# Postnorm attention block on one core: two blocks of row maxima worked in the prologue, and maxima turned on TensorE straight from their columns

## The reference, cut to what matters

```python
def reference(h, gamma, beta, Wq, bq, Wk, bk, Wv, bv, Wo, bo, w_gate, w_up, w_down):
    hn = (h - mean(h)) * rsqrt(var(h) + 1e-05) * gamma + beta      # h: (2, 2048, 256)
    q, k, v = hn @ Wq + bq, hn @ Wk + bk, hn @ Wv + bv             # 16 heads of 64
    q, k = rope(q), rope(k)
    attn = softmax(where(tril, q @ k.T / 8, -inf))                 # per head, 2048 x 2048, causal
    x = layernorm(h + (attn @ v) @ Wo + bo + h)
    return layernorm(x + (silu(x @ w_gate.T / 127) * (x @ w_up.T / 127)) @ w_down.T / 127)
```

## Time and profile before

| | |
|---|---|
| median of 3 runs | 2232.11 us (2231.62 to 2236.57) |
| profiled execution, its own time | 2229.82 us |
| its span, first to last instruction | 2228.0 us |
| mean granted TensorE clock | 0.979 |
| PE busy | 2070.0 us, 93% |
| DVE busy | 1597.6 us, 72% |
| POOL busy | 1391.7 us, 62% |
| ACT busy | 906.6 us, 41% |

### The profile page before, as it was taken

The page is one execution under the profiler, slowest core; times in us unless marked ns, Lnnn a source line. Parts: engine busy times, 40 slices in busy tenths (PEclk is TensorE's granted clock), DMA queues, the critical chain, the costliest instruction groups (busy, mean ns, idle before and its releaser), DMA issues.

```text
span 2228.0 us, 37497 instructions
## 1 busy us (share of the span) xinstructions
PE 2070.0 (93%) x14720; PEld 1287.2 (58%) x14720; DVE 1597.6 (72%) x2262; ACT 906.6 (41%) x1245; POOL 1391.7 (62%) x1204
## 2 busy tenths in 40 slices
PE   6779999999999989999999999999999989889997
PEld 5445555555555545555555555555555545789996
DVE  8576878686878776767777777778787763556654
ACT  4424443444444434434343434343434345434342
POOL 1457777777787866677767777878787879000000
PEclk9899999999999999999999999999999999999999
DMA  6311212121202122122111212121112131231300
GB/s 223 119 30 38 62 39 62 39 62 39 58 25 68 42 68 72 45 65 63 48 53 43 58 43 58 43 58 34 48 34 58 29 119 48 67 104 57 112 10 29
DMA packets 116149, 132.16 MB, mean 59 GB/s; under 512 B 15248, under 2 KB 71184, under 8 KB 115728
## 3 DMA queue, kind: packets, MB, share of 16 engines
q1 hardware_dynamic: 115984, 129.92, 19.5%
HBM read 56.47 MB, written 39.85 MB: 43 GB/s over the span
## 4 chain that ended last, share of the span: by engine, by line
PE 60%; DVE 24%; DMA 5%; SPq 4%; issue 4%; ACT 1%; POOL 1%; ACTq 0%; DVEq 0%
PE o_ps L1239 13%; DVE mpart L833 9%; PE m_ps L1184 7%; DMA rot<-qr 5%; PE s_ps L1205 4%; SPq L385 4%; PE s_ps L1209 4%; PE s_ps L1207 4%; PE s_ps L1211 4%; PE x_ps L1139 3%; DVE qr L860 3%; PE x_ps L1246 3%; DVE qc L871 2%; PE gu_ps L1139 2%; PE gu_ps L1140 2%
## 5 line engine op out<-in xcount | busy, mean ns | idle before, releaser
L542 POOL TENSOR_TENSOR acc<-acc,pt 128x512 f32<-128x512 f32 (+3 forms) x1024 | 1195.8, 1200 | 228.0 <-ACT pt L591 228.0
L591 ACT ACTIVATE pt<-s_ps 128x1024 f32<-128x1024 f32 (+3 forms) x640 | 544.8, 895 | 704.8 <-PE s_ps L1211 342.4
L833 DVE TENSOR_REDUCE mpart<-m_ps 128x2 f32<-128x1024 f32 (+2 forms) x576 | 624.9, 1085 | 288.2 <-PE m_ps L1184 215.7
L1239 PE MATMUL o_ps<-pt,v 128*64 128x512 f32 (+3 forms) x2560 | 547.5, 549 | 0.0
L1184 PE MATMUL m_ps<-qk 64*128 64x512 f32 (+3 forms) x1280 | 290.0, 449 | 85.0 <-DVE mpart L833 73.7
L1184 PEld LDWEIGHTS m_ps<-qk 64*128 64x128 f32 x1280 | 121.1, 185 | 395.6 <-DVE mpart L833 223.6
L1239 PEld LDWEIGHTS o_ps<-pt,v 128*64 128x64 f32 x2560 | 157.8, 138 | 239.1 <-issue 213.8
L537 POOL TENSOR_TENSOR acc<-pt 128x512 f32<-128x512 f32 (+1 forms) x128 | 161.7, 1283 | 193.7 <-ACT pt L591 193.7
L1205 PE MATMUL s_ps<-qk 64*128 64x512 f32 (+3 forms) x1280 | 253.7, 392 | 0.0
L1209 PE MATMUL s_ps<-qk 64*128 64x512 f32 (+3 forms) x1280 | 235.6, 363 | 0.0
L1211 PE MATMUL s_ps<-aux,ones_r 64*128 64x512 f32 (+3 forms) x1280 | 234.7, 362 | 0.0
(11 more groups left out here) (165 smaller groups left out, 2882.0 us busy)
## 6 DMA issues: line engine op xcount, KB each, us to landing
rot<-qr SPq DMA_DIRECT2D x512, 64.0 KB, 2.0
attn<-o_sum SPq DMA_DIRECT2D x64, 256.0 KB, 2.3
o_raw<-attn SPq DMA_DIRECT2D x8, 2048.0 KB, 8.9
v<-v_far SPq DMA_DIRECT2D x16, 768.0 KB, 5.2
v_far<-v_part SPq DMA_DIRECT2D x48, 256.0 KB, 2.0
w_raw<-in_wqkv SPq DMA_DIRECT2D x34, 128.0 KB, 5.1
v_far<-v SPq DMA_DIRECT2D x16, 256.0 KB, 2.4
v<-v_far SPq DMA_DIRECT2D x16, 256.0 KB, 5.0
```

What stands on the lines that cost most here:

```text
L542: nc.gpsimd.tensor_tensor(sums, sums, probs, ALU.add).then_inc(summed, 1)
L591: nc.scalar.activation(pt[:, u % SLOTS, :, q0:NB], s_ps[:, two:two + 2, q0:NB], ACT.Exp, scale=SCALE)\
L833: nc.vector.tensor_reduce(dst, m_ps[:, :, 0:w], AX.X, ALU.max, negate=True).then_inc(maxed, 1)
L1239: last = nc.tensor.matmul(o_ps[rows, q0:NB], v[par][:, j, rows], pt[:, u % SLOTS, a, q0:NB], start=(j == 0), stop=(j == n - 1), skip_group ...
```

## The change

In words: `PROLOGUE_MAXIMA = 12`: the prologue works 12 steps of maxima of the first pair (blocks 0 and 1) in place of 4, and the first pair has 2, 2, 2, 3, 3, 2, 2, 3, 3, 3, 3 left in groups 0 to 10. The first four stand between the v tiles of the last chunk, the other eight between the turns of the second batch's input. In the first pair the third step of a group stands behind the other work, as in the other pairs. The remainders of the prologue (18 instructions) go from DVE to POOL; the rows of batch 1 (16) from POOL to ACT, which needs the negated mean times the inverse deviation (`next_mean`) from DVE. The order of input loads, of PE's chunks and of ACT's steps is changed to fit; ACT loads its first table at once. The copy `spread` and `mz` are gone: `turn_maxima` multiplies by the identity with the column of `mc`, repeated 64 times, as stationary operand, one matmul for each tile and head half, and `ones_r` holds 1/64, since all 64 rows now hold the maximum.

```diff
+PROLOGUE_MAXIMA = 12
+FIRST_COUNT = [2, 2, 2, 3, 3, 2, 2, 3, 3, 3, 3]
...
-                return FIRST_MAXIMA[g]
+                return range(PROLOGUE_MAXIMA + sum(FIRST_COUNT[:g]), PROLOGUE_MAXIMA + sum(FIRST_COUNT[:g + 1]))
...
-            load_input(0)
+            load_input(0, 0)
...
             load_w(0)
+            load_input(0, 1)
             load_wv(0, wv_raw[:, :])
             load_wv(1, v_part[:, :])
+            load_input(0, 2)
+            load_input(0, 3)
...
-            pool.wait_ge(a_rstd, len(STAT_TILES))
-            for t in range(TT):
-                next_rows(t)
+            rest(0)
+            rest(1)
+            rest_wv(0, wv_raw[:, :])
+            rest_wv(1, v_part[:, :])
+            for i in range(2, TURNS):
+                rest(i)
+            for c in range(BLOCKS):
+                remainders(c)
...
+            def next_rows(g):
+                act.wait_ge(next_shift, 1)
+                for t in range(TG * g, TG * (g + 1)):
+                    nc.scalar.activation(h_all[1][:, t, :], h_all[1][:, t, :], ACT.Identity,
+                                         bias=next_mean[:, t:t + 1], scale=rstd[:, TT + t:TT + t + 1])\
+                      .then_inc(next_norm, 1)
...
             rounded(1)
+            next_rows(0)
+            next_rows(1)
             evict_v_first(3)
             rounded(2)
+            shifts(0, 0)
+            next_rows(2)
+            next_rows(3)
+            next_affine(0)
+            next_affine(1)
             rounded(3)
...
-            nc.vector.memset(ones_r[:, :].bitcast(F32), 1.0).then_inc(out_stored, 16)
+            nc.vector.memset(ones_r[:, :].bitcast(F32), 1.0 / DK).then_inc(out_stored, 16)
...
-                    if turns and kind is not FIRST:
-                        spread(it + 1 if g == NG - 1 else it, TURN_M[g])
...
-                    late = 2 if kind is not FIRST else len(ms)
-                    for m in ms[:late]:
+                    for m in ms[:2]:
...
-                    if turns and kind is FIRST:
-                        spread(it + 1 if g == NG - 1 else it, TURN_M[g])
...
             def turn_maxima(n, blk):
-                pe.wait_ge(mz_done, n * BLOCKS + (blk + 1))
+                if blk == 0:
+                    pe.wait_ge(maxed, n * NM + TG)
+                else:
+                    pe.wait_ge(m_rows, n * (TT - TG) + TG * blk)
                 for t in range(TG):
-                    last = nc.tensor.transpose(x_ps[:, t * P:(t + 1) * P], mz[:, t, :], id_f[:, :])
+                    for a, rows in enumerate(halves):
+                        last = nc.tensor.matmul(x_ps[rows, t * P:(t + 1) * P], mc[:, blk, t, a:a + 1].broadcast_to([P, DK]),
+                                                id_f[:, :], start=True, stop=True, skip_group_check=True)
...
+            turn_chunk(0)
+            turn_chunk(1)
+            project_qk(0)
+            for c in range(3):
+                for t in range(TG * c, TG * (c + 1)):
+                    project_v_first(t)
+                if c < 2:
+                    turn_chunk(c + 2)
+                project_qk(c + 1)
             pe.wait_ge(cos_done, 6)
             pe.wait_ge(const_in, 16 * 6)
             for m in range(TG):
-                if m > 0:
-                    pe.wait_ge(maxed, m)
-                maxima(0, 0, m)
-            project_chunk(3)
+                first_maximum(m)
+                project_v_first(3 * TG + m)
             pe.wait_ge(v_done, TT - 1)
             turn_maxima(0, 0)
-            for i in range(TURNS, 2 * TURNS):
-                turn_input(i)
+            for m in range(TG, PROLOGUE_MAXIMA):
+                first_maximum(m)
+                turn_input(TURNS + m - TG)
```

More of the change, by code:

```diff
@@ L458, in _ @@
                 sp.dma_start(dst, src).then_inc(const_in, 16)
-            load_input(1)
+            for g in range(GROUPS):
+                load_input(1, g)
             sp.wait_ge(primed, 1)
@@ L470, in _ @@
                     load_b(1, 1)
+            for done in v_put:
+                sp.wait_ge(done, 16 * BLOCKS)
+            load_v(0, 0, 3, v_in)
             for c in range(BLOCKS):
@@ L688, in rounded @@
                     piece_hi(0, c, a, 0)
+            nc.scalar.activation(pause_act[:, :], ones_f[:, 0:1], ACT.Sqrt)
             root_input(0)
-            root_input(1)
-            weights(0, first=True)
-            root_input(2)
             act.wait_ge(ln_in, 16 * 3)
             affine(0)
+            weights(0, first=True)
             affine(1)
+            root_input(1)
             split_wv(0, wv_raw[:, :])
@@ L911, in pair @@
                 for g in range(NG):
-                    turns = g in TURN_M and (g != NG - 1 or kind is not LAST)
-                    if turns and kind is not FIRST:
-                        spread(it + 1 if g == NG - 1 else it, TURN_M[g])
                     ended = EVICTED.get(g) if g != 1 or kind is not FIRST else None
@@ L939, in pair @@
                         turned_sum(it + 1, *PIECE[g - 1])
-                    for m in ms[late:]:
+                    for m in ms[2:]:
                         maximum(it, m) if m < NM else maximum(it + 1, m - NM)
@@ L967, in turned, with next_means, first_maxima @@
                     turned_sum(0, c, a)
-            def remainders(c):
-                for a in range(2):
-                    piece_lo(0, c, a, 0)
+            def next_means():
+                dve.wait_ge(a_rstd, len(STAT_TILES))
+                nc.vector.scalar_tensor_tensor(next_mean[:, :], mv[:, TT:2 * TT, 0], -1.0, rstd[:, TT:2 * TT],
+                                               ALU.mult, ALU.mult).then_inc(next_shift, 1)
+            def first_maxima(a, b):
+                for m in range(a, b):
+                    maximum(0, m)
             input_group(0)
+            input_rows(0)
             input_group(1)
-            input_rows(0)
+            input_rows(1)
             weights(0)
             input_group(2)
-            input_rows(1)
-            rest(0)
-            rest(1)
-            rest_wv(0, wv_raw[:, :])
-            rest_wv(1, v_part[:, :])
-            input_group(3)
             input_rows(2)
-            rest(2)
-            rest(3)
-            input_rows(3)
             dve.wait_ge(const_in, 16 * 6)
             unturned(0)
+            input_group(3)
+            input_rows(3)
+            turned(0)
+            unturned(1)
             input_group(GROUPS)
             input_group(GROUPS + 1)
-            turned(0)
-            rest(4)
-            rest(5)
-            unturned(1)
+            turned(1)
             input_group(GROUPS + 2)
@@ L998, in _ @@
             input_var(GROUPS)
-            turned(1)
-            rest(6)
-            rest(7)
-            remainders(0)
+            unturned(2)
             input_inv(GROUPS)
-            unturned(2)
-            for m in range(TG):
-                maximum(0, m)
+            next_means()
+            first_maxima(0, 2)
             turned(2)
-            remainders(1)
-            spread(0, 0, first=True)
+            first_maxima(2, TG)
             unturned(3)
+            first_maxima(TG, TG + 2)
             turned(3)
-            remainders(2)
-            remainders(3)
+            first_maxima(TG + 2, PROLOGUE_MAXIMA)
             each_pair(dve, pair)
```

96 lines of the change are left out of this document (44 added, 52 removed).

## The result

The changed kernel takes 2206.57 us (median of 4 runs, 2196.1 to 2210.59) against 2231.86 for the one before: a ratio of 0.9882, interval 0.9849 to 0.9916, 25 us less. The prediction said 2207. Timed again with more runs it took 2202.73 us against 2227.36, ratio 0.9888 (0.9865 to 0.9911). The total agrees with the forecast, but not for the reasons that it gave: two of its terms were off by some 10 us each way, and that they cancel is luck.

The account below looks back on a forecast made before the run. PE bounds the kernel, by its own work in middle pairs, while the first pair loses over 20 us to waits. 5.3 + 15 + 2.4 + 0.5 = 23.2 us off 2229.8 gives 2206.6, said as 2207; 8 in 10 between 2193 and 2224.

Parts of the forecast that it names:

- Part 1: Prologue up to group 1 of the first pair: 5.3 us saved, bounds 0 and 10.
- the walk through the first rows: Start of the prologue, walked by durations: rows at about 14.3 us, first projection at 16.2, 1.3 us earlier.
- sixteen rows on ACT: Prologue: ACT's 16 rows of 256, 0.38 us each, lie beside the eight steps of maxima.
- the late prologue: Rival: POOL's sums or the turned-sum chain delay the first pair to 80 us or later; costs 6 to 8 us, chance 0.13.
- Part 2: First pair, groups 2 to 10: 15 us saved, 75.0 to 60 us, bounds 8 and 21; groups 13 and 15 add 2.4.
- the four steps fewer: First pair, groups 2 to 10: 28 steps become 24, each costing a round of 1.82 us, 7.3 us saved.
- The late step: First pair: third step behind other work saves 4 us of 7.9 at most, plus 2.4 in groups 13 and 15.
- In groups 0 and 1 the four steps: First pair's start: 4 steps instead of 8, some 1.6 us less each, 16.8 us becoming 10.4.
- Part 3: The 64 turns: 23.0 us added on PE, 23.5 given back, 0.5 us saved; bounds 13.5 lost and 12 gained.
- The price of the turn: PE's new turn takes 0.94 to 0.96 us against 0.58: 0.36 us more each, 23 us over 64 turns.
- what comes back there: Turns of blocks 2 and 3, 14 middle pairs: 23.5 us given back by the missing copy, including 9.5 of `qc` waits.
- cover: Turns of blocks 2 and 3: long waits for maxima behind the turn hide its 0.36 us, some 5 us.

Follow-up runs that it names:

- the first trace: The changed kernel, profiled in its fastest run: 2196.1 us, mean clock 0.987.
- copy_back: The changed kernel with DVE's copy and PE's transposes put back, prologue and first pair as changed: 2222.44 us, ratio 0.9961.
- direct_turn: The changed kernel, but DVE's reduction writes the two heads' maxima 64 columns apart and PE turns them with four transposes, no copy: 2187.29 us, ratio 0.9819.
- rest_dve: The changed kernel with the remainders of the input and v weights (10 instructions) back on DVE, those of q and k on POOL: 2204.71 us, ratio 0.9878.
- the second trace: The changed kernel unaltered, run once more and nearer to its usual run: median 2202.73 us (2197.59 to 2209.97).
- four_steps: The changed kernel with 4 steps of maxima in the prologue again, and in groups 0, 1 and 5 all steps ahead of other work: 2217.17 us, ratio 0.9951.
- turn_only: The kernel before with only the turn changed: no DVE copy, PE turns the maxima by eight matmuls: 2210.1 us, ratio 0.9915.

## Why the prediction was right in its total

**Part 1 was wrong.** It forecast the first projection at 16.2 us, the first pair at 73.8 and `weigh` of group 0 at 84.2. It was 19.6, 83.5 and 90.2 in the first trace; in the second 85.7 and 95.2. The steps that failed: the walk through the first rows had no term for what POOL does to DVE (only its rival says "in DVE's way"), and four row steps took 4.01 us beside POOL's sums, 1.38 without them. It named only half a microsecond of ACT's queue, where a root that waits 5.4 to 6.7 us stood ahead of the eviction of chunk 2's v tiles. And it put sixteen rows on ACT at 0.38 us each, beside the path; they took 0.50, and the second eight held PE for 1.99 us. The stages themselves were near: from step 4 to the first pair 18.6 us (67.1 to 85.7) for 16, and from there to `weigh` of group 0 9.5 us for 10.4. None of the three is the whole cause: the row steps alone put right gave nothing in the total, the root's place alone nothing measurable, all together with the late affine step 6.4 us. In place of 5.3 us saved stand some 5 us lost (`weigh` of group 0 at 94.4 to 95.2 us in `copy_back`, `direct_turn`, `rest_dve` and the second trace; only the first trace has 90.2). It was the late prologue that the prediction had as a rival, 6 to 8 us, at 0.13.

**Part 2 was right in mechanism and in its sum, not in its terms.** 75.0 to 60.0 us is the 15 us forecast, in the trace nearest to the usual run. But the four steps fewer gave 11.7 us of it (`four_steps` to the changed kernel) where 7.3 and 2 for the clock stood: the time at half clock in this stretch fell from 11.6 us before to 1.3, where the forecast had a shorter low stretch worth 2 us. The late step gave less than said, 2.7 us by the medians for 6.4 with groups 13 and 15. In groups 0 and 1 the four steps were worth 9.5 us for 6.4.

**Part 3 was wrong: a right price, too little given back, and no clock.** The price of the turn, 0.34 us for 0.36, holds, and at M0 and M1 it is lost in full: 9.4 us for 10.1. At M2 and M3 the forecast comes to 13.4 us gained (9.5, 9 and 5, less 28 x 0.36), and 18.7 were measured. The step that failed is the size of what comes back there, 23.5 us forecast and some 28 measured (18.7 and the price of 28 turns). How it splits between the copy's absence and cover depends on what is changed first: in the kernels with the copy the cover is all of the price, not half, in those without it some 2 us, and the copy's absence gives 27.7 for 18.5. Some 2 us came from other intervals. So the middle pairs gave 11.4 us for 3.3, before the clock. The second omission is the clock itself, 7 to 9 us over the whole kernel by the runs' line: the sum of part 3 has no term for it. Together 0.5 us were forecast and 19 measured in `turn_only`; in the changed kernel the middle pairs show 13.9.

Of the Trainium skill's rule (TensorE: Matmul & The Clock Gate, Terms), that a plain float32 turn lacks the fourfold speed of transpose mode, this case shows less: 0.92 us against 0.58; the records of the two halves start 0.01 us apart, so they run side by side. But `direct_turn` bears out its direction: with transposes and without the copy the kernel is 15 to 19 us faster still.

The account of the second trace closes at 25.5 us: -5.7 up to `weigh` of group 0, 15.0 to that of group 9, 1.4 from there to the second pair, 13.9 in the middle pairs and 0.9 behind them. The forecast had 5.3, 15, 2.4, 3.3, and -2.9 for the eight turns outside the middle pairs.

The signs that the prediction named: turn to `weigh` 0.92 (0.9 to 1.0 said), `qc` waits 2.5 us (none said), maxima 37.9 us (30 said), group 9 at 59.4 us behind group 0 (60 said), group 0 at 90 to 95 (84 said), and the middle pair 1.0 us shorter (within 1 us said). Of those for a failure, the start beyond 80 us occurred.

## What to carry to other kernels

Cost an edit on the bounding engine place by place, not by the number of instructions: the same 0.34 us cost its full price where nothing was waited for behind it and nothing where a wait stood behind it, and once the wait's cause was gone it cost most of its price there too. What each of two edits at one place is worth depends on which is made first; forecast them together. When work moves to an idle engine, look at what the two engines do to each other and at what stands behind its waits in the new queue. When a small instruction takes long, look at what it ends with: DVE's copy took 0.17 us by itself, and the rest of its 0.88 us it stood beside POOL. A total that comes out says little: here some 5 us lost for 5 saved and 14 for 3 in the middle pairs made the forecast come out, and only kernels with one part each showed it.

## What the runs showed of the hardware

- DVE's `tensor_scalar` of 128x256 took 0.40 us alone (1.38 for four in a row). Beside POOL's 128x512 float32 sums (1.26 to 1.31 us) it took 1.15 to 1.35 us and ended 0.15 us behind the sum; with these sums elsewhere four took 1.38 us again.
- DVE's copy of 128x8 took 0.17 us alone, and beside POOL ended 0.03 to 0.04 us behind POOL's instruction, 61 times of 61, so that its mean was 0.88 us.
- A turn of four 128x128 float32 tiles took 0.58 us by transposes and 0.92 us by eight matmuls of 64 columns, two halves at a time.
- In the kernel before each us at 1.2 GHz cost 0.42 us of time, and the runs of one kernel spread by 17 us (2221.7 to 2238.35) mostly with it. A kernel that did more matmul work at its turns had 16 us less of it and took no longer.
- The DMA of `rot`, 128x512 by four transfers, let the sum start 4.6 us behind `qr` in most pairs and 5.3 to 6.3 us in a few, the same five in three kernels with the same middle pairs. Why is open.
